# A fused perceiver on one core: the large attention with its keys in natural layout, its queries prepared during the even batch and its maximum rows in other banks

## The reference, cut to what matters

```python
q_hk = (hidden_q @ Wq.T).reshape(Bv, Sv, H, K)
q_big = jnp.einsum('bshk,hkq->bshq', q_hk, w_kc_q)
q_big = _apply_rope(q_big, sin_q[None, :, None, :], cos_q[None, :, None, :])
kv_r = _apply_rope(kv_c, sin_k[None], cos_k[None])
q_r = jnp.einsum('bshq,hqr->bhsr', q_big, W_qr)
k_r = jnp.einsum('bld,hdr->bhlr', kv_r, W_kr)
scores = jnp.einsum('bhsr,bhlr->bhsl', q_r, k_r)
attn = jax.nn.softmax(scores, axis=-1)
ctx_c = jnp.einsum('bhsl,bld->bhsd', attn, kv_r)
ctx_lat = jnp.einsum('bhsd,hkd->bhsk', ctx_c, w_kc_kv)
ctx = ctx_lat.transpose(0, 2, 1, 3).reshape(Bv, Sv, H * K)
return ctx @ Wo.T
```

## Time and profile before

| what | value |
|---|---|
| median of 3 runs | 3505.46 us (3505.07 to 3515.96) |
| the profiled execution | 3504.15 us, of which its span is 3501.6 us |
| TensorE busy over the span | 2942.5 us (84%) |
| VectorE, ScalarE, GpSimd busy | 2084.2 us (60%), 1277.2 us (36%), 900.8 us (26%) |
| the large attention's loop over batches | first exponential at 763.9 us, last at 2626.4 us |
| mean granted TensorE clock | 0.932 |

### The profile page before, as it was taken

The page is one execution under the profiler, slowest core; times in us unless marked ns, Lnnn a source line. Parts: engine busy times, 40 slices in busy tenths (PEclk is TensorE's granted clock), DMA queues, the critical chain, the costliest instruction groups (busy, mean ns, idle before and its releaser), DMA issues. The chain is left out here.

```text
span 3501.6 us, 51568 instructions
## 1 busy us (share of the span) xinstructions
PE 2942.5 (84%) x17592; PEld 1773.8 (51%) x17592; DVE 2084.2 (60%) x3249; ACT 1277.2 (36%) x2482; POOL 900.8 (26%) x784
## 2 busy tenths in 40 slices
PE   6767734579988988898898889888996889999999
PEld 3544412445544544454455445444543457777776
DVE  3445567357686777677776877686775643333332
ACT  3433312123344343434334433444343333333332
POOL 0001000134354444344434544453440000000000
PEclk9888856679999999999999999999999899999999
DMA  1000030000000000000000000000003000000000
GB/s 39 0 17 0 0 117 0 22 19 10 19 9 19 9 19 9 19 9 19 9 11 17 19 9 9 19 9 19 10 0 145 0 0 0 0 0 0 0 0 25
DMA packets 15045, 57.83 MB, mean 17 GB/s; under 512 B 2512, under 2 KB 7248, under 8 KB 13584
## 3 DMA queue, kind: packets, MB, share of 16 engines
q1 hardware_dynamic: 13392, 53.57, 5.5%
q10 hardware_dynamic: 1600, 3.56, 0.3%
HBM read 55.03 MB, written 2.10 MB: 16 GB/s over the span
## 5 line engine op out<-in xcount | busy, mean ns | idle before, releaser
L917 ACT ACTIVATE cx_prob<-cx_st 128x512 f32<-128x512 f32 (+1 forms) x832 | 477.4, 596 | 742.8 <-PE cx_st L774 680.7
L645 POOL TENSOR_TENSOR cx_acc<-cx_acc,cx_prob 128x512 f32<-128x512 f32 (+1 forms) x352 | 493.8, 1403 | 751.5 <-ACT cx_prob L917 747.4
L1023 DVE TENSOR_REDUCE cx_mhalf<-cx_mx 128x1 f32<-128x804 f32 x512 | 491.2, 983 | 86.5 <-PE cx_mx L747 83.7
L785 PE MATMUL cx_av<-cx_prob,cx_kv 128*64 128x512 f32 (+1 forms) x1664 | 462.2, 635 | 0.0
L773 PE MATMUL cx_st<-cx_q,cx_k 128*128 128x512 f32 (+1 forms) x832 | 372.5, 448 | 84.5 <-ACT cx_prob L917 60.5
L1506 PE MATMUL moe_gu<-moe_wgu,moe_xnT 128*128 128x352 f32 x1280 | 399.0, 463 | 0.0
L1044 DVE TENSOR_TENSOR cx_acc<-cx_acc,cx_prob 128x512 f32<-128x512 f32 (+1 forms) x352 | 371.3, 1055 | 21.7 <-ACT cx_prob L917 19.9
L747 PE MATMUL cx_mx<-cx_k,cx_q 128*128 128x402 f32 x1024 | 309.3, 388 | 53.2 <-DVE cx_mhalf L1023 47.3
L1641 DVE SCALAR_TENSOR_TENSOR moe_hid<-moe_silu,moe_coef,moe_gu 128x176 f32<-128x176 f32 x320 | 127.1, 397 | 351.6 <-ACT moe_silu L1569 349.4
L774 PE MATMUL cx_st<-cx_q,cx_k 128*128 128x512 f32 (+1 forms) x832 | 332.8, 400 | 0.0
L747 PEld LDWEIGHTS cx_mx<-cx_k,cx_q 128*128 128x128 f32 x1024 | 173.4, 195 | 264.0 <-DVE cx_mhalf L1023 216.8
(11 more groups left out here) (214 smaller groups left out, 3945.0 us busy)
## 6 DMA issues: line engine op xcount, KB each, us to landing
cx_ctx<-in_cx_ctxT SPq DMA_DIRECT2D x32, 402.0 KB, 4.3
cx_ctxr<-in_cx_ctxrT SPq DMA_DIRECT2D x32, 402.0 KB, 5.5
moe_wgu<-in_moe_wgu SPq DMA_DIRECT2D x5, 1408.0 KB, 15.3
moe_wd<-in_moe_wd SPq DMA_DIRECT2D x4, 896.0 KB, 25.0
x_all<-in_x SPq DMA_DIRECT2D x1, 2048.0 KB, 5.3
cx_wq<-in_cx_wq SPq DMA_DIRECT2D x1, 2048.0 KB, 12.0
cx_woT<-in_cx_woT SPq DMA_DIRECT2D x1, 2048.0 KB, 29.5
out_x<-x_all SPq DMA_DIRECT2D x1, 2048.0 KB, 7.5
```

What stands on the lines that cost most here:

```text
L645: pool.tensor_tensor(acc[0][rows, :], sofar, prob[slot(kt)][rows, 0, :], ALU.add)\
L785: last = pe.matmul(av[DCX * p:DCX * p + DCX, :], kv[e][0:nk(kt), kt, :], prob[slot(kt)][0:nk(kt), p, :], start=(kt == 0), stop=(kt == NKT ...
L917: act.activation(prob[slot(kt)][rows, p, :], st[p][rows, :], ACT.Exp).then_inc(s_exp, 1)
L1023: dve.tensor_reduce(mhalf[:, i // 2, i % 2:i % 2 + 1], mx[i % 2][:, :, 0:KQ], AX.XY, ALU.max)\
```

## The change

The keys come in natural layout: 128 partitions (keys) by 13 tiles by 64. The rotation on GpSimd, the sum on VectorE (`sum_keys`), the high part on ScalarE (`keep_kh`, into `khl`), the low part on VectorE (`keep_kl`) and the copy for the values (`keep_kv`, now straight from `kr`) each become whole instructions of 128x832. TensorE now transposes the high and low parts together for the scores (`turn_keys`, 13 transposes of 128x128 in four rounds through `misc`), ScalarE stores each round in a new tile `kp`, the maximum scores read `kp`, and two DMAs from SBUF to SBUF (`move`) fill `k1` and `k2`. All this is done two batches ahead, and fetched three ahead, in place of one and two. The queries of the next pair are made in key tiles 7 to 11 of the even batch in place of 0 to 4 of the odd one, and the maximum pieces move to key tiles 1 to 6 (even) and 3 to 9 (odd). The maximum rows go to the two banks of `mx`, both in key tile 11, with no copy awaited between them.

```diff
-    OUT_AT = 4
-    TURN_AT = 6
-    ROWS_AT = NKT - 3
-    SUM_AT = (8, 9, 11, 12)
+    OUT_AT = 5
+    SUM_AT = 4
+    KH_AT = 6
+    KL_AT = 7
+    TURN_AT = 7
+    QUERIES_AT = 7
+    NORM_AT = 10
+    NEGATE_AT = 9
+    ROWS_AT = 11
 
     def pieces(e, kt, third):
 
-        start, end = 3 * (5 if e else 3), 3 * ROWS_AT
+        start, end = (9, 3 * NEGATE_AT + 3) if e else (4, 3 * QUERIES_AT)
         first = lambda k: min(max(0, -(-(k - start) * PIECES // (end - start))), PIECES)
         return range(first(3 * kt + third), first(3 * kt + third + 1))
...
-                fetch(n)
+                sp.dma_start(ctx[:, :, :], a["cx_ctxN"][bass.ds(n, 1), :, :, :]).then_inc(s_ctx, 16)
+                sp.dma_start(ctxr[:, :, :], a["cx_ctxrN"][bass.ds(n, 1), :, :, :]).then_inc(s_ctx, 16)
+
+            def move(n, e):
+
+                sp.wait_ge(s_kp, KROUNDS * (n + 1))
+                if not isinstance(n, int) or n >= 2:
+
+                    sp.wait_ge(s_st, (n - 1) * 2 * NKT)
+                sp.dma_start(k1[e][:, :].bitcast(F32), kp[e][:, 0:SKP].bitcast(F32)).then_inc(s_kd[e], 16)
+                sp.dma_start(k2[e][0:DCX, :].bitcast(F32), kp[e][0:DCX, 0:SKP].bitcast(F32)).then_inc(s_kd[e], 16)
+
...
+                root(1)
+                rotate(2)
+
+            def batch(n, t, e, more, next, far):
                 for kt in range(1, NKT):
                     add(n, kt)
-                    if more and kt % 2 == 1 and 3 <= kt < 3 + 2 * NKC:
-                        rotate(n + 2, kt // 2 - 1)
-                    if more and e == 0 and kt == ROWS_AT:
-                        root(t + 1)
+                    if kt == NORM_AT and far and e == 1:
+                        root(t + 2)
+                    if kt == NORM_AT and far:
+                        rotate(n + 3)
 
...
-            def turn_keys(n, q):
-
-                pe.wait_ge(s_kr, (n + 1) * NKC)
-                if q == 1:
-                    pe.wait_ge(s_kv, 2 * n + 1)
-                for kt in range(8 * q, min(8 * q + 8, NKT)):
-                    o, keys = misc[0:nk(kt), (kt % 8) * DCX:(kt % 8 + 1) * DCX], kr[:, kt * P:kt * P + nk(kt)]
-                    if kt == 8 * q:
-
-                        pe.matmul(o, keys, ident[0:DCX, 0:DCX], start=True, stop=True)
-                    else:
-                        last = pe.transpose(o, keys, ident[0:DCX, 0:DCX])
+            def turn_keys(n, r):
+
+                if r == 0:
+                    pe.wait_ge(s_kl, n + 1)
+                else:
+                    pe.wait_ge(s_kp, KROUNDS * n + r)
+                for kt in range(4 * r, min(4 * r + 4, NKT)):
+                    last = pe.transpose(misc[:, kt % 4 * P:(kt % 4 + 1) * P], khl[:, kt, :, :], ident[:, :])
                 last.then_inc(s_kt, 1)
...
-                    last = pe.matmul(mx[b][:, h, 0:KQ], q, k1[e][:, lo:lo + KQ], start=True, stop=True)
+                    last = pe.matmul(mx[b][:, h, 0:KQ], q, kp[e][:, lo:lo + KQ], start=True, stop=True)
                 last.then_inc(s_mx, 1)
 
             def max_rows(n, p):
 
                 if p == 0:
                     pe.wait_ge(s_nm, n + 1)
-
-                    pe.wait_ge(s_kv, 2 * n + 2)
-                else:
-                    pe.wait_ge(s_rowk, 2 * n + 1)
                 for i in range(4):
                     for part, (w, lo) in enumerate(((nmh, True), (nml, False))):
-                        last = pe.matmul(misc[0:1, i * P:(i + 1) * P], w[:, 4 * p + i:4 * p + i + 1], identb[:, :],
+                        last = pe.matmul(mx[p][0:1, 0, i * P:(i + 1) * P], w[:, 4 * p + i:4 * p + i + 1], identb[:, :],
                                          start=(part == 0), stop=(part == 1))
                 last.then_inc(s_row, 1)
...
-                        if more and e == 1 and third < 2 and kt <= CP // 2:
-                            queries(t + 1, 2 * kt + third)
+                            scores(n + 1, t + e, 1 - e, 0, third)
+                        if more and e == 0 and third < 2 and 0 <= kt - QUERIES_AT <= CP // 2:
+                            queries(t + 1, 2 * (kt - QUERIES_AT) + third)
                         if next:
                             for i in pieces(e, kt, third):
                                 max_scores(t + e, n + 1, 1 - e, i)
+                            if kt == ROWS_AT and third == 1:
+                                max_rows(n + 1, 0)
+                                max_rows(n + 1, 1)
+                    if kt == QUERIES_AT - 1 and more and e == 0:
+                        turn_x(t + 1)
                     if kt == 0 and not is_first(n):
                         denominators(n - 1)
                     if kt == OUT_AT and e == 0 and not is_first(n):
                         out(t - 1)
-                    if kt in (TURN_AT, TURN_AT + 1) and next:
+                    if 0 <= kt - TURN_AT < KROUNDS and more:
                         if kt == TURN_AT and not is_first(n):
 
                             if e == 0:
                                 pe.wait_ge(s_x, t)
                             else:
                                 pe.wait_ge(s_hd, n)
-                        turn_keys(n + 1, kt - TURN_AT)
-                    if kt in (ROWS_AT, ROWS_AT + 1) and next:
-                        max_rows(n + 1, kt - ROWS_AT)
+                        turn_keys(n + 2, kt - TURN_AT)
...
-            def keep_keys(n, e, k, s_k):
-                act.wait_ge(s_kr, (n + 1) * NKC)
+            def keep_kh(n):
+                act.wait_ge(s_kr, n + 1)
+                if not is_first(n):
+
+                    act.wait_ge(s_kt, KROUNDS * n)
+                act.copy(khl[:, :, 0, :].bitcast(F32R), kr[:, :, :]).then_inc(s_kh, 1)
+
+            def keep_kv(n, e):
+                act.wait_ge(s_kr, n + 1)
                 if not isinstance(n, int) or n >= 2:
 
-                    act.wait_ge(s_st, (n - 1) * 2 * NKT)
-                act.copy(k[e][0:DCX, :], kr[:, :]).then_inc(s_k, 1)
-
-            def keep_kv(n, e, q):
-                act.wait_ge(s_kt, 2 * n + q + 1)
-                if q == 0:
-                    if not isinstance(n, int) or n >= 2:
-
-                        act.wait_ge(s_av, (n - 1) * NKT)
-                    act.copy(kv[e][:, 0:8, :], misc[:, :]).then_inc(s_kv, 1)
-                else:
-                    m = nk(NKT - 1)
-                    act.copy(kv[e][:, 8:NKT - 1, :], misc[:, 0:(NKT - 9) * DCX])
-                    act.copy(kv[e][0:m, NKT - 1, :], misc[0:m, (NKT - 9) * DCX:(NKT - 8) * DCX]).then_inc(s_kv, 1)
+                    act.wait_ge(s_av, (n - 1) * NKT)
+                act.copy(kv[e][:, :, :], kr[:, :, :]).then_inc(s_kv, 1)
+
+            def keep_turned(n, t, e, r):
+
+                act.wait_ge(s_kt, KROUNDS * n + r + 1)
+                if r == 0 and (not isinstance(n, int) or n >= 2):
+
+                    act.wait_ge(s_kd[e], 32 * t)
+                w = P * (min(4 * r + 4, NKT) - 4 * r)
+                act.copy(kp[e][:, 4 * r * P:4 * r * P + w], misc[:, 0:w]).then_inc(s_kp, 1)
...
-            def sum_keys(n, c):
-                cols = slice(c * KC, (c + 1) * KC)
-                dve.wait_ge(s_rope, n * NKC + c + 1)
-                if c == 0 and not is_first(n):
-
-                    dve.wait_ge(s_k2, n)
-                    dve.wait_ge(s_kt, 2 * n)
-                    dve.wait_ge(s_kl, n)
-                dve.tensor_tensor(kr[:, cols], ctx[:, cols], ctxr[:, cols], ALU.add).then_inc(s_kr, 1)
-
-            def keep_kl(n, e):
-                dve.wait_ge(s_k1, n + 1)
-                dve.wait_ge(s_kr, (n + 1) * NKC)
-                dve.tensor_tensor(k1[e][DCX:P, :], kr[:, :], k1[e][0:DCX, :].bitcast(F32), ALU.subtract)\
-                    .then_inc(s_kl, 1)
-
-            def normalise(t, base):
+            def sum_keys(n):
+                dve.wait_ge(s_rope, n + 1)
+                if not is_first(n):
+
+                    dve.wait_ge(s_kv, n)
+                dve.tensor_tensor(kr[:, :, :], ctx[:, :, :], ctxr[:, :, :], ALU.add).then_inc(s_kr, 1)
+
+            def keep_kl(n):
+                dve.wait_ge(s_kh, n + 1)
+                dve.tensor_tensor(khl[:, :, 1, :], kr[:, :, :], khl[:, :, 0, :], ALU.subtract).then_inc(s_kl, 1)
...
-                        if third < 2 and more and e == 1 and kt < CP // 2:
-                            rotate(t + 1, 2 * kt + third)
+                        if third < 2 and more and e == 0 and 0 <= kt - QUERIES_AT < CP // 2:
+                            rotate(t + 1, 2 * (kt - QUERIES_AT) + third)
                         if next:
                             for i in pieces(e, kt, third):
                                 reduce_max(n + 1, i)
                     if kt == 0 and e == 0:
                         odd_queries(t)
-                    if kt == 1 and next:
-                        keep_kl(n + 1, 1 - e)
+                    if kt in (1, 2) and more and e == 1:
+                        split(t + 1, kt - 1)
```

(18 more changed lines are left out.)

170 lines of the change are left out of this document (94 added, 76 removed).

## The result

The changed kernel takes 3560.2 us (median of four runs, 3548.0 to 3564.5) against 3509.5 us of the kernel before, run beside it: a ratio of 1.014, 95% interval 1.010 to 1.017. It is slower by some 50 us. The forecast was 3548.

A forecast was written before the change was run, and what follows sets the result against it. Bounds: TensorE under queries, VectorE under maximum pieces, ScalarE at batch starts. Pair 122.5 us, 3.0 more: +45 over fifteen pairs, preparation +3, shorter late batch -4, so +44 on 3504.15: 3548 us, range 3517 to 3585.

The forecast's parts named there:

- The pair: Two batches: 74.2 + 47.3 = 121.5 us, 122.5 with collisions, 3.0 us more than before; fifteen pairs give +45 us.
- The ends: Preparation ahead of the loop turns two batches' keys, +3 us; the late even batch without queries is about 4 us shorter.
- Even batch: 74.2 us: VectorE's chain of 26.4 us exceeds TensorE's 23.3 in key tiles 1 to 6, last reduction ending at 32.6.
- Odd batch: 47.3 us: first reduction at 12.15; TensorE reaches the transposes at 28.7 and waits 3.2, VectorE runs dry for 1.8.
- rival 3: Clearly slower: whole-key instructions collide, sums take 1.4 us, TensorE's clock falls after the new stall; pair 126, 3600 us; chance 0.13.
- The low part's waits: TensorE's transposes wait for VectorE's low part of the keys: 3.2 us in the odd batch, 1.15 in the even.
- The queries' place: Reciprocals and heads of the even batch leave the queries' cover and stand between VectorE's reductions: 4.2 us.
- The rows: Key tiles 10 to 12 of the odd batch gain 2.2 us, 7.8 against 10.0.
- GpSimd late: GpSimd's two remaining sums end about 3.1 us into the even batch; denominators (2.05 before) and the scores behind them wait.
- Rival 1: Faster: collisions vanish and the low part is ready in time; pair 115 to 118, 3437 to 3482 us; chance 0.20.
- Rival 2: No change: losses some 3 us a pair smaller, through free sums and an early low part; 3495 to 3515 us; chance 0.13.
- Rival 4: DMAs into `k1` come late and each batch waits for them; 1 us a batch is +30; chance 0.02.

The follow-up runs named there:

- e4: The kernel before with only the maximum rows changed: both in key tile 11, in the two banks of mx; 3448.9 us.
- e5: The changed kernel with queries back in odd-batch key tiles 0 to 4, pieces as before, key transposes from key tile 8 instead of 7; 3418.9 us.
- e1: The changed kernel with TensorE's four rounds of key transposes in key tiles 8 to 11 instead of 7 to 10; 3481.9 us.
- e11: The changed kernel with the keys' high and low parts one key tile earlier (5 and 6), the sum kept at 4; 3504.7 us.
- e3: The changed kernel with queries back in key tiles 0 to 4 of the odd batch and maximum pieces placed as before; 3506.5 us.
- e6: The changed kernel with each reciprocal of the denominators on 16 columns instead of 256; 3494.5 us.
- e7: The kernel before with each reciprocal of the denominators on 16 columns instead of 256; 3471.1 us.
- e8: The changed kernel with GpSimd's key products in key tile 8 instead of 10 and key transposes from key tile 8 instead of 7; 3504.2 us.
- e2: The changed kernel with GpSimd's two products for the keys in key tile 8 instead of 10; 3635.1 us.
- e9: The changed kernel with the keys' sum, high part and low part one key tile earlier (3, 5, 6 instead of 4, 6, 7); 3557.5 us.
- e10: e5 with the keys' sum, high part and low part one key tile earlier (3, 5, 6 instead of 4, 6, 7); 3485.3 us.

## Why the forecast held

The kernels form a chain from the kernel before to the changed one, in us a pair: 119.5, less 3.6 for the maximum rows (e4), less 2.0 for natural keys, whole instructions and the longer hand-overs with slack (e4 to e5), plus 4.2 for the queries in the even batch (e5 to e1), plus 4.9 for the hand-over that is a key tile too early (e1 to the changed kernel; 2.5 of it is the low part's slack by e11): 123.0. The sizes hold along this path only; without the queries' move the later hand-over is worth 6.3 (e3 to e5). The 2.0 is a remainder: nothing inside it was tried alone.

- **The pair.** Forecast 122.5, of which 121.5 was the sum of the two batches and 1.0 for collisions; measured 123.0. Odd batch 47.3 forecast and 47.36 measured, even batch 74.2 and 75.5.
- **The ends.** The spans of the two profiled executions are 61.1 us apart (3501.6 and 3562.7). Fifteen pairs make 52. From the first fetch of keys to the first exponential it is 80.7 us (694.3 to 775.0) where it was 76.7 (687.2 to 763.9): +4.0, forecast +3. The loop from the first to the last exponential grew by 47.5 us, 4.5 less than the fifteen pairs: forecast -4. The other 9.6 us lie ahead of the fetch and behind the loop, in stages that the change leaves alone; the first fetch comes between 672 and 694 us in these kernels.
- **Even batch.** The odd queries end at 4.6 us (4.35 forecast), the first reduction starts at 6.3 (6.2), the last ends at 34.6, where I had 32.6. The step that was mis-sized is VectorE's chain of 26.4 us, which took 28.3: the keys' sum met GpSimd and took 1.98 us instead of 1.05, VectorE waited 0.6 us for the second piece, which the sum did not have, and 2.6 (2.4) at the output product. What follows took 0.7 us less than forecast; TensorE waited 1.04 us for the low part (1.15).
- **Odd batch.** First reduction at 12.1 us (12.15). TensorE came to the transposes at 28.9 (28.7) and waited 2.0 us (3.2), VectorE stood for 2.7 (1.8). That the batch ended on time to 0.1 us is luck: the half clock behind the wait, which I had put into rival 3 and not into the sum, made up for the shorter wait.
- **The low part's waits.** 3.2 + 1.15 = 4.35 forecast, 3.0 as a wait on TensorE, 4.9 as what a pair lost against the later hand-over (e1), 2.5 against the earlier low part (e11).
- **The queries' place.** I had 4.2 us for reciprocals and heads that come out from under the queries; the whole move costs 4.2 (e5 against e1), but it holds more than that. The reciprocals themselves account for 2.2 (e6 less e7) where I had 3.5; the rest is not tried apart. The waits say where it sits: in e1 TensorE waits 7.0 us a pair for reductions (82.4 us in 11.8 pairs), 1.6 at x's turn and 0.7 for the denominators; in e5 4.0 (49.6 in 12.3), none and none, but 0.8 for the maxima.
- **The rows.** 2.2 us forecast for key tiles 10 to 12 of the odd batch, 3.6 a pair for both batches (e4).
- **GpSimd late.** The wait of the denominators is there (1.46 us), but the products in key tile 8 give nothing back (e8).
- **The rivals.** Rival 1 made the low part's being ready in time its condition, and e1 meets it: 118.1 us a pair and 3481.9 us, at the upper edge of its 3437 to 3482. With the queries left alone as well (e5) the kernel is faster than that rival had it, 3419 us. Rival 2 asked for losses 3 us a pair smaller, which e11 has (120.5), and the changed kernel not. Rival 3's half clock behind the new wait did come, in the odd batch, but a pair loses only 1.8 us by the clock, 1.6 before; it is large in four neighbours (e2, e3, e9, e10). Rival 4, late transfers: no such wait.

## What to carry to other kernels

A hand-over between two engines needs slack in the queue of the engine that makes it, not only in time: here a hand-over one key tile later was worth 4.9 us a pair, some 73 us of 3560 in fifteen pairs, more than the whole change cost. When several edits go in together, time each alone: the two that helped (-5.6 us a pair) were hidden by two that hurt (+9.1). And when work is moved earlier on a full queue, look at what stands behind it: the same wait was cured by TensorE later, by the low part alone earlier, and by sum and low part earlier, and a pair gained 4.9, 2.5 and nothing.

## What the hardware showed beside that

TensorE's clock carries part of this. After waits of about 2 us it stood at half (0.50), for 3 to 4 us in the changed kernel (1242.5 to 1245.5 and a like stretch in each pair), but for some 7 us in e9 (1231 to 1238) behind a wait that was no longer (2.00 and 2.02). Kernels that differ in nothing but a place differ by it: e9 and e11 in one key tile for the keys' sum, with a clock loss of 5.2 and 2.4 us a pair, the changed kernel and e2 in the place of GpSimd's products, with 1.8 and 6.9. What makes one stretch twice as long as another is open. The cost of it is argued by subtraction; no run holds the clock still.

VectorE's low part takes 1.01 us alone and, in e2, 1.82 to 1.91 beside a GpSimd product, in every one of 22 instances. With the keys in whole instructions the running sums cost less in the mean (873 ns, 1053 in the earlier trace rows), but one meeting costs more: with products of 832 columns 0.8 us for the low part and 1.5 for the running sum of e2's rows, and 0.9 for the changed kernel's keys' sum at 1282.34, beside a running sum of GpSimd.
